# Attention block with a routed FFN on one core: the second batch's rotation moved to GpSimd, and the edges of stages and the end reordered

## The chip, the cores and the metric

One core of one Trainium2 chip. The time is the device time of one execution in microseconds (us), all loads, stores and on-chip work included. The engines are named as the profile names them: PE (TensorE matmuls) and PEld (its weight loads), DVE (VectorE), ACT (ScalarE), POOL (GpSimd) and SP (SyncE, which only issues DMAs here; SPq is its queue of DMA-issuing instructions).

## What is computed

Two batches of 1,024 tokens of width 128 go through attention (16 heads of 8 elements, rotary embedding, causal), a layer norm, a routed FFN of 4 experts (top 2) and a second layer norm, all in float32.

```python
Q = rope((x @ qw).reshape(batch, seq, 16, 8)); K = rope((x @ kw)...); V = (x @ vw)...
score = einsum('bhqd,bhkd->bhqk', Q, K) / sqrt(8); score = score - 1e10 * (1 - causal)
score = score - max(score); attn = einsum('bhqk,bhkd->bhqd', softmax(score), V)
x = layernorm(x + attn.reshape(batch, seq, 128) @ ow)
gates = top-2 of softmax(x @ router_w + router_b), renormalised
h = silu(x @ w1[e]) * (x @ w3[e]);  out = sum over e of gates[:, e] * (h @ w2[e])
x = layernorm(x + out)
```

## The kernel before

**Stages.** There are eight groups of four heads: groups 0 to 3 are the first batch, 4 to 7 the second. Stage s computes the score maxima of group s (40 "S" units, a matmul on PE followed by a row maximum on DVE) while the exponentials and the weighted sum of group s-1 run: "T" units are the transposed scores (PE), read by an exponential on ACT (L696) and, on the diagonal, a causal select on POOL (L574); "PV" units are the products with V (PE). Stage 0 (PROLOGUE) also holds part of its own group's T and PV. Stage 1 is FIRST, stages 2 to 7 follow STEADY_ORDER, and stage 8 (LAST) has no S. The order within a stage is one list of steps that all engines walk: in STEADY_ORDER `s`, `t`, `p`, `m`, `n` are an S, T, PV, MROWS and NORM step. Every engine executes its own part in that order and waits on semaphores.

**Maxima.** The maxima must be subtracted inside the T matmul. POOL splits them into three bf16 parts (split_max), PE turns them (MROWS), DVE copies them into max_rows, and SP sends them by four DMAs into extra rows of q_op (send_rows, L442). The first T unit of that half of the queries waits on these DMAs (rows_loaded). S units pass through a ring of three PSUM banks, so PE can be at most three units ahead of DVE.

**Projection and rotation.** x arrives in four chunks of 512 tokens, two for each batch. For each chunk q and k are projected (n = 0 to 7; n = 4 to 7 are the second batch). For each n, DVE multiplies the two projections by cosine and sine (turns_of), POOL adds them (sum_of_turns, L509), ACT writes the first bf16 part (first_part), DVE subtracts it (first_rest, L810), ACT writes the second (second_part), and POOL makes the third (third_part, L502). SP stores the parts, three DMAs for each n (L420), to a scratch area in DRAM in the six-fold form in which the groups load them (load_q, load_k). For n = 4 to 7 this is done by the steps P between the S units of the prologue, with the second batch's V.

**The end of attention and the FFN.** During LAST, steps C run the first layer norm and the router for chunk 0 (function between). For chunks 1 to 3 they are spread over the previous chunk's experts. An expert unit (16 for each chunk) is six matmuls of the two input products, silu on ACT, the product on DVE, a split of the hidden values into a high part (ACT) and a low part (POOL, L610), and three matmuls of the output product (L1206). The last layer norm and a store of 512 tokens close each chunk.

## Time and profile before

| | us |
|---|---|
| median of 3 runs | 436.07 |
| the three runs | 436.11, 432.88, 436.07 |
| the profiled execution, device time | 432.75 |
| its span in the trace | 430.7 |
| busy in the span: PE / DVE / ACT / POOL | 391.1 / 315.1 / 265.1 / 193.5 |

The profiled execution took 432.75 us, 2.05 us more than its span, and 3.3 us less than the median of the runs. By the trace, stage 0's last maxima are joined on DVE at 60.5 us, stage 7's at 241.7 us, the experts begin at 269.4 us and the last matmul of the FFN's products ends at 421.7 us. A row of the timeline gives the start, the duration, the engine and line, the operation, what it writes and reads, the count of merged instructions, and in brackets the idle time of the engine before it with what ended it. PEclk is TensorE's granted clock as a share of 2.4 GHz: 0.50 is 1.2 GHz.

### The profile page before, as it was taken

The numbers are of one execution on the slowest core, as the hardware profiler recorded it, in microseconds if no ns is written. First come the engines' busy times: TensorE is split into PE (matmuls) and PEld (weight loads), VectorE is DVE, ScalarE is ACT, GpSimd is POOL, SyncE is SP. The second block draws the span as 40 slices with busy tenths as digits, with TensorE's granted clock in tenths as the row PEclk, the third lists the DMA queues.
The fourth block names the chain that finished last, engine by engine and source line by source line (L and its number), as shares of the span: only waits on it lengthen the run. The fifth ranks groups of instructions, "written<-read, shape, count | busy, mean of one in ns | idle before, by whom it ended". The sixth has DMA issues, their size and how long they took to land.

```text
span 430.7 us, 7532 instructions
## 1 busy us (share of the span) xinstructions
PE 391.1 (91%) x2420; PEld 202.9 (47%) x2420; DVE 315.1 (73%) x1027; ACT 265.1 (62%) x377; POOL 193.5 (45%) x256
## 2 busy tenths in 40 slices
PE   4658769999999999999999888999999999999991
PEld 2243122232323323233232331788887887888770
DVE  3659888999999999999999543346576658656653
ACT  1233615687786867778687886566665656665550
POOL 7627611261343515235261322466565646655661
PEclk9959686999999999999999998999999999999996
DMA  6474841322213122131210000000000000000000
GB/s 216 153 203 91 286 115 23 75 53 57 52 22 89 39 70 51 25 93 22 74 35 3 1 3 2 0 2 1 2 1 24 2 1 24 2 1 3 24 0 24
DMA packets 45244, 21.13 MB, mean 49 GB/s; under 512 B 30995, under 2 KB 42899, under 8 KB 45206
## 3 DMA queue, kind: packets, MB, share of 16 engines
q1 hardware_dynamic: 44950, 20.47, 18.2%
q8 instruction: 19, 0.31, 0.3%
q10 hardware_dynamic: 256, 0.20, 0.2%
q14 instruction: 19, 0.16, 0.1%
HBM read 13.11 MB, written 7.35 MB: 47 GB/s over the span
## 4 chain that ended last, share of the span: by engine, by line
PE 70%; DVE 9%; ACT 5%; DMA 4%; issue 4%; POOL 3%; SPq 3%; ACTq 0%; POOLq 0%; DVEq 0%
PE o_bank L1127 14%; PE t_bank L1195 9%; PE bank L1084 9%; PE bank L1195 9%; PE t_bank L1206 9%; PE t_bank L1109 8%; PE small_bank L1084 5%; DMA q_op<-max_rows 3%; SPq L442 3%; ACT num L696 2%; DVE num L912 2%; POOL roped L509 1%; DVE num L985 1%; DVE x_w L850 1%; PE o_bank L1214 1%
## 5 line engine op out<-in xcount | busy, mean ns | idle before, releaser
L696 ACT ACTIVATE num<-t_bank 128x1024 f32<-128x1024 f32 (+2 forms) x160 | 142.8, 939 | 60.4 <-PE t_bank L1109 59.7
L610 POOL TENSOR_TENSOR hid_lo<-num,q_op 128x512 fp32r<-128x512 f32 x64 | 83.0, 1300 | 61.2 <-ACT q_op L749 60.0
L574 POOL TENSOR_SCALAR_AFFINE_SELECT num<-num 128x512 f32<-128x512 f32 x64 | 40.1, 636 | 120.7 <-ACT num L696 120.7
L1084 PE MATMUL bank<-k_op,q_op 128*128 128x512 bf16 (+7 forms) x256 | 71.8, 339 | 11.4 <-DMA q_op<-q_scratch 7.1
L1127 PE MATMUL o_bank<-num,v_op 128*32 128x512 f32 (+3 forms) x768 | 81.5, 503 | 0.1
L749 ACT ACTIVATE q_op<-num 128x512 fp32r<-128x512 f32 x64 | 40.5, 632 | 45.0 <-DVE num L985 44.5
L854 DVE TENSOR_REDUCE maxima<-bank 128x1 f32<-128x512 f32 x86 | 57.0, 684 | 2.6 <-PE bank L1084 1.6
L1109 PE MATMUL t_bank<-q_op,k_op 64*128 64x512 bf16 (+3 forms) x384 | 49.6, 337 | 4.3 <-ACTq L677 1.7
L1084 PEld LDWEIGHTS bank<-k_op,q_op 128*128 128x128 bf16 x256 | 21.2, 99 | 63.6 <-DVE maxima L854 23.4
L985 DVE TENSOR_TENSOR num<-bank,num 128x512 f32<-128x512 f32 x32 | 22.1, 691 | 30.7 <-ACT num L756 30.5
L850 DVE CUSTOM_DVE_ANT_0 mg_w<-bank,resid 128x256 f32<-128x256 f32 (+7 forms) x92 | 39.3, 447 | 4.7 <-PE bank L1084 3.8
L985 DVE TENSOR_TENSOR num<-t_bank,num 128x512 f32<-128x512 f32 x32 | 22.1, 690 | 27.3 <-ACT num L756 24.5
L1084 PE MATMUL small_bank<-k_op,q_op 128*128 128x512 bf16 (+6 forms) x128 | 38.7, 331 | 1.4 <-DVE maxima L854 1.1
L850 DVE CUSTOM_DVE_ANT_0 x_w<-small_bank,resid 128x64 f32<-128x64 f32 (+7 forms) x86 | 36.5, 443 | 3.4 <-PE small_bank L1084 1.6
L850 DVE CUSTOM_DVE_ANT_0 mg_t<-bank,resid 128x320 f32<-128x320 f32 (+7 forms) x78 | 35.1, 466 | 2.5 <-PE small_bank L1084 1.0
L1109 PEld LDWEIGHTS t_bank<-q_op,k_op 64*128 64x128 bf16 x384 | 13.9, 94 | 38.0 <-issue 15.5
L854 DVE TENSOR_REDUCE maxima<-small_bank 128x1 f32<-128x512 f32 x42 | 28.7, 683 | 1.3 <-PE small_bank L1084 0.9
L1127 PEld LDWEIGHTS o_bank<-num,v_op 128*32 128x32 f32 x768 | 15.9, 108 | 25.7 <-issue 22.4
L1195 PE MATMUL bank<-q_op,w_hi 128*128 128x512 f32 x64 | 26.8, 419 | 0.0
L1206 PE MATMUL t_bank<-q_op,w_hi 128*128 128x512 f32 x64 | 25.4, 396 | 0.9 <-POOL hid_lo L610 0.9
L1195 PE MATMUL t_bank<-q_op,w_hi 128*128 128x512 f32 x64 | 25.7, 401 | 0.2 <-DVE num L985 0.2
L1206 PE MATMUL t_bank<-hid_lo,w_hi 128*128 128x512 f32 x64 | 25.4, 397 | 0.0
(142 smaller groups left out, 629.2 us busy)
## 6 DMA issues: line engine op xcount, KB each, us to landing
q_op<-q_scratch SPq DMA_DIRECT2D x64, 48.0 KB
w_raw<-in_w_all SPq DMA_DIRECT2D x6, 512.0 KB, 4.0
k_op<-k_scratch SPq DMA_DIRECT2D x60, 48.0 KB, 1.9
xT<-in_x_feat SPq DMA_DIRECT2D x4, 256.0 KB, 5.9
q_op<-max_rows SPq DMA_DIRECT2D x64, 3.0 KB
out_tokens<-num SPq DMA_DIRECT2D x4, 256.0 KB, 2.3
q_scratch<-num SPq DMA_DIRECT2D x2, 384.0 KB, 2.8
k_scratch<-num SPq DMA_DIRECT2D x2, 384.0 KB, 2.8
```

Source lines behind the costliest of these rows:

```text
L574: pool.affine_select(out=tile, in_=tile, compare_op=ALU.is_ge, fill=0.0, base=0, pattern=[[0, GH], [1, P]], channel_multiplier=-1)\
L610: pool.tensor_tensor(hid_lo[:, m % HB, :], hid[:, m % HB, :], hid_hi[:, m % HB, :].bitcast(F32), ALU.subtract).then_inc(f_lo, 1)
L696: act.activation(num[:, t % PB, :, off:CH].rearrange("p (k i) t -> p i k t", i=2)[:, :, h:h + each, :], t_bank[k % TB][:, :, 0:each * (CH ...
L749: act.activation(hid_hi[:, m % HB, :], hid[:, m % HB, :], ACT.Copy).then_inc(f_hi, 1)
L850: ins = dve.tensor_tensor_reduce(masked_s[job % SB][:, at], ring(s, step)[:, at], causal[:, CH - width:CH], 1.0, LOWEST, ALU.add, ALU.max, ...
L854: ins = dve.tensor_reduce(maxima[:, half, pr, j:j + 1], ring(s, step)[:, at], AX.X, ALU.max)
L985: dve.tensor_tensor(hid[:, n % HB, :], bank[2 * (n % 2) + 1][:, :], silu_sb[:, n % 2, :], ALU.mult).then_inc(f_hid, 1)
L1084: ins = pe.matmul(ring(s, step)[:, i * width:(i + 1) * width], q_op[u][:, pr, j, :, :].rearrange("p i q -> p (i q)"), k_op[u][:, pr, lo:lo ...
L1109: ins = pe.matmul(t_bank[k % TB][:, i, (pr - h) * width:(pr - h + 1) * width] .rearrange("p (j q) -> p j q", q=QB), k_op[w][rows, pr, kt * ...
L1127: ins = pe.matmul(o_bank[h * QD:(h + 1) * QD, off:CH], v_op[w][:, kt, h, :], num[:, t % PB, h, off:CH], start=kt == 0, stop=kt == TI * (c ...
L1195: ins = pe.matmul(bank[2 * (n % 2) + w][:, :], ws[:, at], xs[ch], start=k == 0, stop=k == 2)
L1206: ins = pe.matmul(bank[4 + e % 2][:, :], ws[:, at], hs[:, m % HB, :], start=f == 0 and k == 0, stop=f == FT - 1 and k == 2)
```

## The change

- The rotation of n = 4 to 7 no longer uses DVE. ACT copies both projections to SBUF (copy_turns), and POOL alone does the seven operations that follow (late_block): two products, a sum, two casts and two subtractions. Each of these 28 is placed behind a given S unit of stage 0 (13) or stage 1 (15) by LATE_AT. For n = 0 and 1 the sum and the third part go from POOL to DVE.
- The projections of n = 4 and 5 and two of the V products come ahead of the prologue's first S unit, those of n = 6 and 7 and the last V product behind S units 5, 9 and 3.
- The stores of n = 4 to 7 go from the prologue to stage 2: six DMAs behind load_q in the middle, six at its end. x_tok is loaded at the end of stage 3 (it was in stage 0) into x_res, which serves as the buffer of late_block until then.
- FIRST has an order of its own; the prologue's T and PV units are two S units later. The tables' first half is loaded by ACT's queue.
- In LAST the copies that ACT made for steps C (L720, L726, L729, L733) are made by DVE, and L736's by POOL. The first three expert units (E) stand ahead of the last NORM.
- In the output product the matmul that reads the low part comes last of three. In the last chunk DVE makes the last low part; the last expert's copy, transposes and sum are done in halves; the last normalisation is shared by DVE and POOL, and its store by SP and ACT.

```diff
-PROJ_AT = (12, 14, 16, 18, 20)
-T_AT, PV_AT = (22, 24, 25, 27, 28, 30), (29, 31, 33, 35)
-V_AT = (3, 7, 11)
+PROJ_AT = (5, 9)
+V_AT = 3
+T_AT, PV_AT = (25, 27, 28, 30, 31, 33), (31, 33, 35, 37)
+LATE_STEPS = 7
+LATE_AT = [(0, at) for at in (2, 4, 6, 8, 14, 16, 18, 20, 22, 24, 29, 32, 36)] \
+    + [(1, at) for at in (2, 4, 6, 8, 10, 12, 14, 16, 18, 21, 24, 27, 30, 33, 36)]
-        plan.append(("NORM", NC - 1))
+        plan += [("E", n) for n in range(E_LAST)] + [("NORM", NC - 1)]     # E_LAST = 3
+FIRST_ORDER = "ssssmssssnsssststsstsstsssttsspssttsspmsttssspssttsspssttsspssnttppp"
-FIRST = steady_plan(STEADY_ORDER.replace("t", "", SEG_T[0] - T_END[0]).replace("p", "", TI), done=TI - 1)
+FIRST = steady_plan(FIRST_ORDER, done=TI - 1)
...
             def stage(plan, s, u, load=False):          # on sync
...
                         load_q(sp, s + 1, v, 0, range(GH))
+                        if s == 2:
+                            store(PROJ_FIRST)
+                            store(PROJ_FIRST + 1)
...
                         load_q(sp, s + 1, v, 1, range(GH))
                         load_k(sp, s + 1, v, 1)
+                        if s == 2:
+                            store(PROJ_FIRST + 2)
+                            store(PROJ_FIRST + 3)
+                        if s + 1 == NG:
+                            sp.dma_start(x_res[:, :, :], x_tok.rearrange("(t p) d -> p t d", p=P)).then_inc(ld_res, 16)
...
+            def late_block(k):                          # on gpsimd
+                n, r = PROJ_FIRST + k // LATE_STEPS, k % LATE_STEPS
+                at = n - PROJ_FIRST
+                cols = slice(n // 2 % NC * CH, (n // 2 % NC + 1) * CH)
+                by_cos, by_sin = late_turn[at]
+                if r == 0:
+                    pool.wait_ge(late_turned, at + 1)
+                    ins = pool.tensor_tensor(by_cos, by_cos, cos_sb[:, cols], ALU.mult)
+                if r == 1:
+                    ins = pool.tensor_tensor(by_sin, by_sin, sin_sb[:, cols], ALU.mult)
+                if r >= 2:
+                    pool.wait_ge(late_step, k)
...
+                if r == 2:
+                    ins = pool.tensor_tensor(by_cos, by_cos, by_sin, ALU.add)
+                if r in (3, 5):
+                    ins = pool.tensor_copy(rope_part(n, (r - 3) // 2), by_cos)
+                if r == 4:
+                    ins = pool.tensor_tensor(by_cos, by_cos, rope_part(n, 0), ALU.subtract)
+                if r == 6:
+                    ins = pool.tensor_tensor(rope_part(n, 2), by_cos, rope_part(n, 1), ALU.subtract)
...
+            def copy_turns(n):                          # on scalar
+                act.wait_ge(proj_ready, n + 1)
+                pair, at = 3 + 2 * (n % 2), n - PROJ_FIRST
+                act.activation(late_turn[at][0], bank[pair][:, :], ACT.Copy)
+                act.activation(late_turn[at][1], bank[pair + 1][:, :], ACT.Copy).then_inc(late_turned, 1)
...
+            copy_v(0)
+            copy_v(1)
+            first_part(2)
+            act.wait_ge(parts_stored[0], 2 * PARTS * 16)
+            act.wait_ge(ops_filled, 2)
+            load_k(act, 0, 0, 0)
+            second_part(2)
+            first_part(3)
+            copy_v(2)
+            act.wait_ge(ld_small, 16 * 2)
+            act.activation(ident_b[:, :], ident[:, :], ACT.Copy).then_inc(ident_cast, 1)
+            copy_turns(4)
+            second_part(3)
+            copy_turns(5)
+            copy_v(3)
...
             turns_of(0)                                 # on vector
-            for n in range(1, PROJ_FIRST):
+            sum_of_turns(0)
+            turns_of(1)
+            first_rest(0)
+            sum_of_turns(1)
+            third_part(0)
+            first_rest(1)
+            third_part(1)
+            for n in range(2, PROJ_FIRST):
                 turns_of(n)
-                first_rest(n - 1)
+                if n > 2:
+                    first_rest(n - 1)
...
+                if first and r == 0:                    # between(), on vector; r 1, 7 and 8 alike
+                    dve.wait_ge(job_read, SB + LAST_JOBS)
+                    dve.wait_ge(c_mgt, 1 + ch)
+                    dve.tensor_copy(mg_w[:, :].rearrange("p (i g r) -> p i g r", i=TI, g=NG),
+                                    merged[:, 1:1 + NG, 0:TI, :].rearrange("p g i r -> p i g r")).then_inc(c_mg, 1)
...
                     if f == 0:                          # experts(), on tensor
                         pe.wait_ge(f_eo, ch * E + e + 1)
-                    pe.wait_ge(f_lo, ch * UNITS + m + 1 + HB)
+                    pe.wait_ge(f_hi, ch * UNITS + m + 1)
                     at = slice(2 * E * F + m * P, 2 * E * F + (m + 1) * P)
-                    for k, (ws, hs) in enumerate(((w_hi, hid_hi), (w_hi, hid_lo), (w_lo, hid_hi))):
+                    for k, (ws, hs) in enumerate(((w_hi, hid_hi), (w_lo, hid_hi), (w_hi, hid_lo))):
+                        if k == 2:
+                            pe.wait_ge(f_lo, ch * UNITS + m + 1 + HB)
```

**SP's queue, the end of stage 2 and the start of stage 3.** Before, the maxima's rows (q_op<-max_rows) follow the loads for the next group at once:

```order
L378 DMA q_op<-zeros 3x8x64
L385 DMA k_op<-k_scratch 48x512 x4
L442 DMA q_op<-max_rows 3x8x64 [waits job_read]
L442 DMA q_op<-max_rows 3x8x64 x3
L374 DMA q_op<-q_scratch 48x8x64 [waits t_ready]
```

And now, at the same place:

```order
L406 DMA k_op<-k_scratch 48x512 x4
L442 DMA q_scratch<-by_sb 128x3x512 [waits late_ready]
L442 DMA q_scratch<-by_sb 128x2x512 [waits late_ready]
L442 DMA q_scratch<-roped 128x512 [waits late_ready]
L442 DMA k_scratch<-by_sb 128x3x512 [waits late_ready]
L442 DMA k_scratch<-by_sb 128x2x512 [waits late_ready]
L442 DMA k_scratch<-roped 128x512 [waits late_ready]
L464 DMA q_op<-max_rows 3x8x64 [waits job_read]
L464 DMA q_op<-max_rows 3x8x64 x3
```

Six stores of the second batch's last two blocks stand between the loads and the rows.

**POOL in stage 0, from the V layout to the first causal select.** Before (neg_max to max_part are the five small operations of split_max):

```order
L521 COPY v_op<-v_tok 128x32x8 [waits v_copied,v_cleared]
L539 TENSOR_SCALAR neg_max<-maxima 128x16 [waits job_read]
L540 CAST max_part<-neg_max 128x2x8 [waits split_step]
L541 TENSOR_TENSOR rest<-neg_max,max_part 128x16 [waits split_step]
L542 CAST max_part<-rest 128x2x8 [waits split_step]
L543 TENSOR_TENSOR max_part<-rest,max_part 128x2x8 [waits split_step]
L509 TENSOR_TENSOR roped<-by_sb 128x512 [waits split_step,part_ready2,turned]
L509 TENSOR_TENSOR roped<-by_sb 128x512 [waits part_ready2,turned]
L502 TENSOR_TENSOR x_res<-roped,x_res 128x512 [waits part_ready1]
```

Now:

```order
L576 COPY v_op<-v_tok 128x32x8 [waits v_copied,v_cleared]
L542 TENSOR_TENSOR x_res<-x_res,turns_sb 128x512 [waits late_turned]
L544 TENSOR_TENSOR x_res<-x_res,turns_sb 128x512
L550 TENSOR_TENSOR x_res<-x_res 128x512 [waits late_step]
L552 CAST x_res<-x_res 128x512 [waits late_step]
L594 TENSOR_SCALAR neg_max<-maxima 128x16 [waits job_read]
L595 CAST max_part<-neg_max 128x2x8 [waits split_step]
L596 TENSOR_TENSOR rest<-neg_max,max_part 128x16 [waits split_step]
L597 CAST max_part<-rest 128x2x8 [waits split_step]
L598 TENSOR_TENSOR max_part<-rest,max_part 128x2x8 [waits split_step]
L554 TENSOR_TENSOR x_res<-x_res 128x512 [waits split_step,late_step]
```

Four of POOL's new operations stand ahead of the first split of maxima, and none of them waits for DVE.

**PE at the end of LAST.** Before, the NORM's transposes (ident, o_sb), which wait for ACT's copy of the output, stand ahead of the experts:

```order
L1127 MATMUL o_bank<-num,v_op 32x128 [waits masked,t_exped]
L1127 MATMUL o_bank<-num,v_op 32x128 x3
L1146 MATMUL small_bank<-ident,o_sb 128x128 [waits job_read,o_copied]
L1146 MATMUL small_bank<-ident,o_sb 128x128 x3
L1195 MATMUL bank<-q_op,w_hi 128x512 [waits c_top,f_hid,c_lo]
```

Now the experts follow the last PV at once, and the transposes come behind three units of them:

```order
L1256 MATMUL o_bank<-num,v_op 32x128 [waits masked,t_exped]
L1256 MATMUL o_bank<-num,v_op 32x128 x3
L1330 MATMUL bank<-q_op,w_hi 128x512 [waits c_top,f_hid,c_lo]
L1330 MATMUL bank<-k_op,w_hi 128x512
L1330 MATMUL bank<-q_op,w_lo 128x512
```

## Rows read from the trace of the kernel before

**Rows 1.** Busy time by stretch: start:end, length, then each engine's busy (instructions).

```profile
60.50:86.50 26.00, 23.67 (x134) 6.66 (x134) 23.04 (x82) 12.82 (x14) 5.06 (x15) 0.80 0.30 75
86.50:112.30 25.80, 25.57 (x206) 8.16 (x202) 24.15 (x88) 19.50 (x23) 9.88 (x20) 1.00 0.25 54
241.80:269.40 27.60, 23.11 (x199) 8.54 (x198) 10.01 (x40) 21.76 (x30) 7.21 (x14) 0.94 0.01 2
269.40:421.70 152.30, 149.98 (x711) 121.10 (x709) 90.29 (x255) 92.82 (x162) 88.88 (x70) 1.00 0.02 6
```

**Rows 2.** Timeline of PE in stages 0, 1 and 3.

```profile
25.07 0.50 PE L1084 MATMUL bank<-k_op,q_op 128*128 128x64 bf16 x4 [7.13 <-DMA q_op<-q_scratch]
...
47.41 0.61 PE L1109 MATMUL t_bank<-q_op,k_op 64*128 64x512 bf16 x2 [1.74 <-ACTq L677]
...
62.21 0.30 PE L1136 MATMUL bank<-ident_b,max_part 128*48 128x128 bf16 x1 [2.05 <-POOLq L544]
...
119.52 0.61 PE L1109 MATMUL t_bank<-q_op,k_op 64*128 64x512 bf16 x4 [0.20 <-DMA q_op<-max_rows]
```

**Rows 3.** Timeline of DVE in stage 0.

```profile
13.10 1.61 DVE L810 TENSOR_TENSOR roped<-roped,num 128x512 f32<-128x512 f32 x1 [0.28 <-ACT num L654]
...
34.18 0.69 DVE L823 TENSOR_TENSOR by_sb<-t_bank,turns_sb 128x512 f32<-128x512 f32 x1
...
60.47 0.17 DVE L860 TENSOR_TENSOR maxima<-maxima 128x16 f32<-128x16 f32 x1
```

**Rows 4.** Timeline of POOL in stage 0.

```profile
11.13 1.27 POOL L509 TENSOR_TENSOR roped<-by_sb 128x512 f32<-128x512 f32 x1 [2.73 <-DVE by_sb L824]
...
17.89 1.15 POOL L502 TENSOR_TENSOR num<-roped,num 128x512 bf16<-128x512 f32 x1 [1.29 <-ACT num L650]
...
34.07 0.40 POOL L521 COPY v_op<-v_tok 128x256 f32<-128x256 f32 x1 [7.02 <-ACT v_tok L645]
```

**Rows 5.** Timeline of SP's DMA queue in stages 0, 3 and 4.

```profile
28.98 1.88 SPq L374 DMA_DIRECT2D q_op<-q_scratch  x4
...
40.67 3.12 SPq L442 DMA_DIRECT2D q_op<-max_rows  x4
...
113.06 1.72 SPq L385 DMA_DIRECT2D k_op<-k_scratch  x4
115.37 2.98 SPq L442 DMA_DIRECT2D q_op<-max_rows  x4
...
141.20 2.98 SPq L442 DMA_DIRECT2D q_op<-max_rows  x4
```

**Rows 6.** Issues of one line: count, then ns min/median/max of one.

```profile
L420 SPq DMA_DIRECT2D k_scratch<-num x6: 333/359/443, 17.0 to 27.1; - x6
```

**Rows 7.** One transfer in the view of DMA issues: KB each, us to landing.

```profile
x_res<-in_x_tok SPq DMA_DIRECT2D x1, 0.5 KB, 6.4
```

**Rows 8.** Single microseconds of Rows 1's view; last three: granted clock, DMA share, GB/s.

```profile
61.00:62.00 1.00, 0.00 (x0) 0.00 (x0) 0.39 (x4) 0.00 (x0) 0.72 (x4) 0.50 1.07 350
71.00:72.00 1.00, 1.00 (x8) 0.36 (x7) 1.00 (x2) 0.73 (x2) 0.40 (x1) 0.90 0.00 0
```

**Rows 9.** Timeline of PE in LAST.

```profile
245.39 0.66 PE L1166 MATMUL bank<-ident,mg_w 128*128 128x128 f32 x4 [1.36 <-ACT mg_w L720]
...
257.36 1.06 PE L1182 MATMUL bank<-rw,x_tw 128*128 128x4 f32 x8 [0.99 <-ACT x_tw L733]
...
269.00 0.66 PE L1146 MATMUL small_bank<-ident,o_sb 128*128 128x128 f32 x4 [0.71 <-ACT o_sb L705]
```

**Rows 10.** Waits from 272 to 420 us: total us, times, longest.

```profile
PE small_bank L1171 <- ACT mg_t L726: 1.1, 2, 0.6
```

**Rows 11.** Timeline of POOL, then of DVE, at the end.

```profile
419.39 1.27 POOL L610 TENSOR_TENSOR hid_lo<-num,q_op 128x512 fp32r<-128x512 f32 x1 [0.80 <-ACT q_op L749]
...
423.16 1.13 DVE L997 SCALAR_TENSOR_TENSOR num<-o_bank,gates,num 128x128 f32<-128x128 f32 x4 [3.48 <-PE o_bank L1214]
...
426.87 1.11 DVE L912 TENSOR_SCALAR num<-num,mv,rstd 128x128 f32<-128x128 f32 x4 [1.20 <-POOL rstd L614]
```

225 lines of the change are left out of this document (142 added, 83 removed).

## Prediction

> **What bounds the kernel now.** I read the busy time by stretch first, since the share over the whole span mixes stages with different limits. In a steady stage PE is busy 25.57 of 25.80 us, with DVE close behind at 24.15 [rows 1]. Nothing in stages 2 to 7 can gain unless PE's own work shrinks, and it doesn't. The experts are the same: PE 149.98 of 152.30 us [rows 1]. Time is open in four places. Stage 0 lasts to 60.5 us; its first score matmul waits 7.13 us for the loads of q, to 25.07, and its first T unit starts at 47.41 [rows 2]. In stage 1, PE is busy 23.67 of 26.00 us at a mean granted clock of 0.80 [rows 1], and DVE 23.04. In LAST, PE is busy 23.11 of 27.60 us [rows 1], and the waits named there are for ACT [rows 9]. At the end, a chain of short steps follows the last matmul [rows 11].
>
> **Stage 0, start.** The first rotation is a chain that passes from DVE to POOL, ACT, DVE, ACT and POOL. A sum takes 1.27 us on POOL [rows 4]; DVE operations of that size take about 0.68 [rows 3], except where one with two SBUF inputs met POOL's: 1.61 [rows 3]. Moving the two sums and third parts to DVE saves about 0.6 for the first sum, 0.5 for each third part, and the slowed subtraction; step by step I get the last part of n = 1 at 17.0 us instead of 19.0 (it began at 17.89 and took 1.15 [rows 4]). But ACT's queue now has two V copies and first_part(2) ahead of load_k, and first_part(2) waits for turns that DVE makes 2 us later than before. So k's loads move only from 20.8 to about 20.2, and the first S comes 0.6 us earlier, not 2. The fourth n is no earlier: second_part(3) stands behind copy_turns(4).
>
> **Stage 0, middle.** The four P steps with DVE work cost DVE 4 x 2 x 0.61 for turns (0.69 in the row, overlapping the next by 0.08 [rows 3]) and 4 x 0.7 for the subtractions, 7.7 us in all, between S units. That is removed. It does not become 7.7 us of gain, because of SP. From 28.98 us on SP issues six groups of four loads with no gap, each about 1.9 us, and reaches the maxima's rows at 40.67 [rows 5]. Nothing in the change shortens this: the loads start when n = 3 is stored, at 29.0 as before. The last row is issued at about 43.8 and lands 1.2 us later (in stage 3, 115.37 + 2.98 = 118.35, and PE starts at 119.52 [rows 2, 5]). So the first T unit can't start before 45.0. I expect PE and DVE to be through S25 at about 41.3 and to stall for 3.7 us; the T unit then starts at 45.0 instead of 47.41 with two S units more behind it (1.3 us). Together with a little idle time less behind, S40 is read at 56.1 instead of 60.5 [rows 3]: **-4.4 us**, with 0 and -7 as the ends (nothing; all 7.7 but 0.7).
>
> **POOL's 28 new operations.** 20 have two inputs, 1.15 to 1.27 us each [rows 4]; 8 are casts, which the trace has only smaller: 0.40 for 256 elements [rows 4], and at most a two-input operation's 1.15. I take 0.65, near twice 0.40 less the fixed part. The sum is 20 x 1.2 + 8 x 0.65 = 29 us. From 27.3 us to the end of stage 1 there are about 53 us, with 12 us of other work for POOL (5.06 in stage 1 [rows 1] and about as much again, with V and the selects, in stage 0). 41 of 53 fits, and most blocks wait for nothing, so POOL runs ahead of its place. They are hidden: 0 us. DVE's S operations read PSUM and one SBUF tile, as its turns do, and those kept 0.69 us [rows 3].
>
> The Trainium skill (SBUF — State Buffer, "Who interferes with whom") says that a DVE operation holds up GpSimd's reads where both its inputs are in SBUF. The row of 1.61 us agrees; by that rule the S units leave POOL alone, which keeps the rival on POOL below small.
>
> **Stage 1.** MROWS behind four S units instead of two hides PE's 2.05 us wait for POOL's split [rows 2], since S3 and S4 give DVE about 1.3 us more to do meanwhile. T starts after S12, when its rows (4.2 us from the copy) have landed. DVE then bounds the stage: 23.04 us of work [rows 1], 0.55 for the NORM moved in, some 1 of unavoidable gaps. 26.2 becomes about 24.5: **-1.7** (0 to -2.5).
>
> **The moved stores.** In the middle of stage 2 SP has time for six more issues. At its end it has not. A store's issue takes 0.36 us [rows 6], 0.41 with its gap, so six take 2.5 us. SP had 0.59 us free between the end of load_k (113.06 + 1.72) and the rows at 115.37 [rows 5], and then 0.20 us of PE waiting was left at the T unit [rows 2]: PE was already waiting for these rows. So everything beyond 0.59 is added: **+2.0** (0 to +4, as 1.57 MB, two n of six copies of 128 x 512 x 2 bytes, also move at the 350 GB/s that the row of 61 us shows, 4.5 us [rows 8]). PE has nothing later to win it back from.
>
> In stage 4 x_tok's load stands at the same place. By issue alone it would cost 0.3 us: one issue of up to 0.9, less 0.59. But it takes 6.4 us to land [rows 7]. Issued at 140.6 it lands at 147.0; the rows, issued at 141.20 [rows 5], landed by the pattern of stage 3 at 145.3. I take **+1.5** (+0.3 to +2.5), near the later bound, because 1 MB spreads over all DMA engines ahead of the rows.
>
> The Trainium skill (DMA: Bandwidth & Descriptors, "Queues, rings and completion order") says that on each engine the descriptors of a queue are consumed in ring order. By it the rows start only behind x_tok's data, 1.7 us late; without it, 0.3. No row of this trace has the two back to back.
>
> **LAST.** PE waits 1.36 us for the copy of mg_w, 0.99 for x_tw and 0.71 for the output's copy [rows 9], 3.06 us; ACT makes those copies between exponentials. DVE is busy 10.01 of 27.60 us [rows 1] and takes its copies at once. ACT loses 3 us of work. The other waits make up the 4.5 us of PE's idle time; some turn into waits for exponentials. Without the 0.71, which belongs to the next step: **-3.4** (-2 to -5; the last 1.6 is what its mean clock of 0.94 lost over 27.6 us [rows 1]). E ahead of NORM removes the 0.71 wait, and silu and the first product follow earlier; NORM's transposes are still executed: **-0.9** (-0.5 to -1.3).
>
> **Experts.** The order of three matmuls is worth nothing where PE is saturated. The move of mg_t's copy in front of the hidden split removes PE's 1.1 us [rows 10]: **-0.8** (0 to -1.1).
>
> **End.** The last low part took POOL 419.39 to 420.66 [rows 11]; on DVE it is 0.69 behind a sum, to 420.4, and the matmul that needs it is now the third: -0.8. Halves let the sum of 1.13 us [rows 11] start about 0.65 earlier. The last normalisation, 1.11 us [rows 11], becomes 0.56 beside POOL's half, at -0.5 with the shorter stores: **-2.0** (-1.2 to -2.6).
>
> **Sum.** -4.4 - 1.7 + 2.0 + 1.5 - 3.4 - 0.9 - 0.8 - 2.0 = -9.7 us, against the profiled execution's 432.75: 423.05. The median of the runs is 3.3 us above that execution, with nothing in one trace to say why. I put the same difference on the median: 436.07 - 9.7 = **426.4**. A difference of 1% (4.4 us) is about what a measurement of this kernel can tell from none.
>
> **Rivals.**
> - *Half clock after the stalls in stages 3 and 4.* In stage 1 PE idled 2.05 us and the clock was at half from 61 to 71 us [rows 2, 8]. There DVE set the pace, so it cost little; in a stage where PE is busy 99% ten such microseconds cost up to 5. Against it: waits of 1.36 and 0.99 us in LAST cost only a share of 0.06 [rows 1]. One such fall: 426.4 + 5 = 431.4. Chance 0.15, for 429 to 434.
> - *Stage 0 gains nothing.* The longer stall puts PE at half clock (after waits of this kind it was there at 61 us [rows 8]) and the T units crawl: 426.4 + 4.4 = 430.8. Chance 0.08. For it: T can start only 2.4 us earlier. Against: DVE has 9 us of S units left there, at any clock.
> - *POOL becomes the bound: the slower side.* The place is stages 0 and 1: selects and splits stand behind the new blocks, and PV and the rows wait for them. 53 - 12 = 41 us are free, 1.47 a block; beyond that mean each block's excess is paid 28 times. From 1.97 a block it costs 14 us and eats all of the gain and 1% more: 440. For it: an addition took 1.61 on DVE against POOL [rows 3], so slow meetings exist; against: POOL's own rows are at 1.15 to 1.27. Chance 0.04.
> - *More than the sum.* Fewer waits keep PE at full clock in stages 0 and 1 and in LAST, which has 1.6 us at stake, and stage 4's load doesn't delay the rows: 422. Chance 0.13.
>
> The forecast has 0.60, for 423 to 430. The range leaves out a tenth on each side at most: it takes in rival four (less its tail) and most of the first two, 419.5 to 432. Faster by over 1% (below 431.7): 0.59 of the forecast, 0.13, 0.07 and 0.06 of the first two, 0.85. Within 1%: 0.11. Slower: 0.04.
>
> **What would show it.** Right: T's first unit at 45 us behind a PE wait of 3 to 4 us for q_op<-max_rows; DVE's join of stage 0 at 56; PE waits of about 2 us for q_op<-max_rows in stages 3 and 4 and none elsewhere; no PE wait for mg_w or x_tw in LAST; the experts beginning some 4 us sooner after stage 7's join. Wrong: a T unit in stage 0 that waits for ACT or POOL, POOL busy over 9 tenths there, or no wait in stage 3, which would put the time some 3 us lower.

## The result and the profile after

The changed kernel took 430.98 us, the median of ten executions from 430.11 to 432.40. The kernel before took 435.37 us beside it, the median of ten from 432.88 to 436.18. The ratio is 0.9924, with a 95% interval from 0.9900 to 0.9948. The change is a gain of 3.3 us by the ratio (the two medians alone lie 4.4 us apart), under the 1% that the prediction named as the bound of "faster". The forecast was 426.4.

The profiled execution took 431.6 us with a span of 429.9 and a mean clock of 0.962 (before: 432.75, 430.7 and 0.955). The spans of the two traces therefore differ by only 0.8 us. This small difference is made of large gains and large losses that stand against each other. To see it, I cut both traces at the same events: the instruction of DVE that joins the maxima of a stage (L860 before, L961 after), and the first matmul of the experts.

```
stretch                                before    after   change   predicted
start to join of stage 0                60.47    59.29    -1.18        -4.4
stage 1                                 26.21    24.67    -1.54        -1.7
stage 2                                 25.84    25.62    -0.22         0
stage 3                                 25.82    30.50    +4.68        +2.0
stage 4                                 25.83    30.46    +4.63        +1.5
stages 5 to 7                           77.55    77.50    -0.05         0
join of stage 7 to first expert matmul  27.70    23.20    -4.50        -3.4, and -0.9 for E
first expert matmul to the end         161.28   158.66    -2.62        -0.8 and -2.0
sum                                                       -0.80        -9.7
```

Two notes on the table. A second trace of the changed kernel (after_p1, below) divides the first two rows differently, with 2.3 us gained in stage 0 and 0.7 in stage 1; their sum is the firmer number, 2.7 us here and 3.1 there. And the first expert matmul now stands ahead of NORM's transposes, which took 0.4 us before it (269.00 [rows 9] to 269.42), so 0.4 of the 4.50 us has only moved into the last row.

These are the stretches of the changed kernel in the columns of [rows 1], and two of stage 0 where the first T unit stands:

```profile
40.00:48.00 8.00, 1.66 (x7) 0.37 (x6) 1.91 (x7) 0.83 (x1) 1.98 (x2) 0.66 0.24 51
48.00:54.00 6.00, 6.00 (x32) 1.26 (x34) 3.64 (x10) 3.79 (x6) 3.03 (x5) 0.60 0.01 0
59.30:83.96 24.66, 23.04 (x132) 7.24 (x138) 23.48 (x86) 12.93 (x15) 20.63 (x30) 0.86 0.18 42
109.58:140.08 30.50, 26.31 (x201) 8.19 (x202) 24.45 (x88) 19.71 (x24) 9.89 (x20) 0.94 0.35 97
140.08:170.54 30.46, 26.34 (x201) 8.15 (x202) 24.44 (x88) 19.71 (x24) 9.89 (x20) 0.94 0.33 80
248.05:271.24 23.19, 21.35 (x195) 8.23 (x194) 12.59 (x44) 18.39 (x24) 7.77 (x15) 1.00 0.01 2
271.24:421.06 149.82, 149.52 (x712) 121.77 (x712) 90.62 (x256) 93.91 (x163) 87.60 (x69) 1.00 0.02 6
```

Read the third row first. POOL is at 20.63 us in stage 1, where it had 5.06 [rows 1], and yet the stage is shorter: DVE's 23.48 us fill it. Then the fourth and fifth: PE did the work of a steady stage in 30.5 us; it was busy for 26.3 of them, a part of that at half clock. In the first row, all engines are mostly idle together, from 40 to 48 us. Who is late, the timeline of PE names (it answers to [rows 2]):

```profile
46.52 0.61 PE L1238 MATMUL t_bank<-q_op,k_op 64*128 64x512 bf16 x2 [6.34 <-DMA q_op<-max_rows]
...
61.06 0.30 PE L1265 MATMUL bank<-ident_b,max_part 128*48 128x128 bf16 x1 [0.60 <-POOLq L599]
...
120.05 0.60 PE L1238 MATMUL t_bank<-q_op,k_op 64*128 64x512 bf16 x4 [3.88 <-DMA q_op<-max_rows]
...
150.48 0.60 PE L1238 MATMUL t_bank<-q_op,k_op 64*128 64x512 bf16 x4 [3.81 <-DMA q_op<-max_rows]
```

The last of these rows is the third wait for the same kind of transfer, in stage 4. The wait for POOL's split has become 0.60 us from 2.05 [rows 2]. All three large waits end with the transfer of the maxima's rows, so the next view is SP's queue (it answers to [rows 5]):

```profile
42.04 3.11 SPq L464 DMA_DIRECT2D q_op<-max_rows  x4
...
110.11 1.71 SPq L406 DMA_DIRECT2D k_op<-k_scratch  x4
111.87 0.96 SPq L442 DMA_DIRECT2D q_scratch<-by_sb  x2
112.87 0.72 SPq L442 DMA_DIRECT2D q_scratch<-roped  x1
113.64 1.24 SPq L442 DMA_DIRECT2D k_scratch<-by_sb  x2
114.92 0.95 SPq L442 DMA_DIRECT2D k_scratch<-roped  x1
115.91 2.96 SPq L464 DMA_DIRECT2D q_op<-max_rows  x4
...
142.54 1.80 SPq L507 DMA_DIRECT2D x_res<-in_x_tok  x1
144.39 3.67 SPq L464 DMA_DIRECT2D q_op<-max_rows  x4
```

The six moved stores keep SP from 111.87 to 115.87. Counted from the join before them, the rows are issued 6.33 us later (115.91 - 109.58), and before the change it was 2.85 us (115.37 - 112.52) [rows 5]. In stage 4 one load holds the queue for 1.80 us, and then the four rows take 3.67 us to issue instead of 2.98 [rows 5]. After the wait of stage 3 the granted clock falls to the lower of its two levels, 1.2 GHz, for three microseconds (single microseconds, last three columns clock, DMA share, GB/s):

```profile
120.00:121.00 1.00, 0.95 (x6) 0.23 (x6) 0.00 (x0) 0.52 (x1) 0.00 (x0) 1.00 0.54 85
121.00:122.00 1.00, 1.00 (x9) 0.20 (x8) 0.98 (x3) 1.00 (x2) 0.20 (x1) 0.52 0.47 72
...
123.00:124.00 1.00, 1.00 (x7) 0.22 (x9) 0.79 (x6) 0.55 (x1) 0.58 (x2) 0.50 0.08 16
```

The stage is 4.68 us longer and its wait 3.68 us longer than before (3.88 less the 0.20 in [rows 2]): the clock's share is 1.0 us.

POOL's new operations, grouped by line from 20 to 84 us (busy us, mean ns, then idle time before them), cost about what was estimated (1.2 us for an operation with two inputs, 0.65 for a cast):

```profile
L544 POOL TENSOR_TENSOR by_sb<-by_sb,turns_sb 128x512 f32<-128x512 f32 x2 | 2.5, 1272 | 0.0
...
L552 POOL CAST by_sb<-by_sb 128x512 bf16<-128x512 f32 x4 | 2.4, 610 | 0.2
```

The end of the changed kernel (it answers to [rows 11]) has DVE's half, POOL's half and the store that follows POOL's:

```profile
425.84 0.66 DVE L1010 TENSOR_SCALAR num<-num,mv,rstd 128x128 f32<-128x128 f32 x2 [1.19 <-POOL rstd L670]
```

```profile
425.91 1.65 POOL L675 TENSOR_SCALAR num<-num,mv,rstd 128x128 f32<-128x128 f32 x2 [0.18 <-POOL rstd L670]
```

```profile
427.60 0.41 ACTq L861 DMA_DIRECT2D out_tokens<-num  x1
```

A tile of the normalisation takes 0.83 us on POOL and 0.28 on DVE (1.11 for four [rows 11]). The last row but one is thus the longer half, and it sets when the output leaves.

### The profile page after: what moved, and what is told of

The parts are those of the page before. It is cut to its first block, busy times and chain, and to the rows that moved or that the text cites. A ratio compares the mean times of both kernels' runs of the same rounds, so it can differ in the third digit from the quotient of the medians.

```text
span 429.9 us, 7520 instructions
## 1 busy us (share of the span) xinstructions
PE 387.0 (90%) x2398; PEld 202.4 (47%) x2420; DVE 311.4 (72%) x1022; ACT 262.0 (61%) x373; POOL 207.7 (48%) x274
## 4 chain that ended last, share of the span: by engine, by line
PE 70%; DVE 11%; SPq 6%; DMA 5%; issue 3%; ACT 2%; POOL 2%; ACTq 0%; POOLq 0%; DVEq 0%
PE o_bank L1256 13%; PE bank L1330 10%; PE t_bank L1330 10%; PE t_bank L1343 10%; PE bank L1215 8%; PE t_bank L1238 7%; PE small_bank L1215 4%; DMA q_op<-max_rows 3%; SPq L464 3%; DVE mg_w L951 2%; DVE x_w L951 2%; DVE maxima L955 2%; DVE mg_t L951 2%; PE o_bank L1352 2%; SPq L406 1%
## 5 line engine op out<-in xcount | busy, mean ns | idle before, releaser
L666 POOL TENSOR_TENSOR hid_lo<-num,q_op 128x512 fp32r<-128x512 f32 x63 | 81.7, 1301 | 57.9 <-ACT q_op L825 56.7
L1215 PE MATMUL bank<-k_op,q_op 128*128 128x512 bf16 (+7 forms) x241 | 66.0, 332 | 4.3 <-DMA q_op<-q_scratch 1.6
L955 DVE TENSOR_REDUCE maxima<-bank 128x1 f32<-128x512 f32 x83 | 55.5, 685 | 3.7 <-PE bank L1215 2.5
L951 DVE CUSTOM_DVE_ANT_0 x_w<-small_bank,resid 128x384 f32<-128x384 f32 (+7 forms) x82 | 35.8, 454 | 8.3 <-PE small_bank L1215 6.7
L1215 PE MATMUL small_bank<-k_op,q_op 128*128 128x512 bf16 (+7 forms) x121 | 37.6, 338 | 2.8 <-DVE maxima L955 0.9
L951 DVE CUSTOM_DVE_ANT_0 mg_t<-bank,resid 128x448 f32<-128x448 f32 (+7 forms) x80 | 35.8, 464 | 2.9 <-PE small_bank L1215 1.4
L955 DVE TENSOR_REDUCE maxima<-small_bank 128x1 f32<-128x512 f32 x45 | 30.8, 684 | 8.2 <-PE small_bank L1215 7.3
L1330 PE MATMUL t_bank<-q_op,w_hi 128*128 128x512 f32 x64 | 25.7, 401 | 0.0
L1215 PEld LDWEIGHTS small_bank<-k_op,q_op 128*128 128x128 bf16 x127 | 11.2, 98 | 30.7 <-DVE maxima L955 10.1
```

What stands on the lines that cost most here:

```text
L666: pool.tensor_tensor(hid_lo[:, m % HB, :], hid[:, m % HB, :], hid_hi[:, m % HB, :].bitcast(F32), ALU.subtract).then_inc(f_lo, 1)
L951: ins = dve.tensor_tensor_reduce(masked_s[job % SB][:, at], ring(s, step)[:, at], causal[:, CH - width:CH], 1.0, LOWEST, ALU.add, ALU.max, ...
L955: ins = dve.tensor_reduce(maxima[:, half, pr, j:j + 1], ring(s, step)[:, at], AX.X, ALU.max)
L1215: ins = pe.matmul(ring(s, step)[:, i * width:(i + 1) * width], q_op[u][:, pr, j, :, :].rearrange("p i q -> p (i q)"), k_op[u][:, pr, lo:lo ...
L1330: ins = pe.matmul(bank[2 * (n % 2) + w][:, :], ws[:, at], xs[ch], start=k == 0, stop=k == 2)
```

## Experiments

**The theory** after the traces: the change did what it set out to do on every engine, and lost most of it on SP's queue. At three places DMA issues stand in order ahead of the rows that PE waits for: the loads of group 1 in stage 0, six stores in stage 3, one load in stage 4. **The rivals**: the data of those transfers and not the order of the issues (it is under way beside the rows wherever the issues stand); the clock; and that another engine would be late next, so that no edit of the queue gives more than a part.

**One cause at a time.** Three kernels, each the changed one with one edit. Only the kernel before ran beside each of them, so a difference from the changed kernel's 430.98 us is one between series; the stages in the traces are the firmer reading. The first moves the stores of blocks 6 and 7:

```
 if step == ("T", 1, 0, 0, 0):            # stage 3
-    wait parts_stored[2], parts_stored[3]
+    wait parts_stored[2]
     load_q(sp, s + 1, v, 0, range(GH))
+    if s + 1 == NG: store(PROJ_FIRST + 2); store(PROJ_FIRST + 3)
 if step == ("END",):
+    if s + 1 == NG: wait parts_stored[3]
     load_q(...); load_k(...)
-    if s == 2: store(PROJ_FIRST + 2); store(PROJ_FIRST + 3)
```

> The changed kernel with the six stores of blocks 6 and 7 moved from the end of stage 2, where the rows of stage 3 queue behind them (rows issued at 115.91 us, a PE wait of 3.88 us, half clock behind it, stage 3 taking 30.5 us and not 25.8), to the middle of stage 3 behind the q loads. Theory A: the lateness of the rows is what stage 3 costs, all of it. Then stage 3 reads 25.9 us, the wait falls to about 0.4 us, and the kernel ends 4.7 us earlier: 426.3 us, 0.9815 of before. Rival B: SyncE's queue is as late as before with the stores gone, since the q and k loads of stage 4 already fill it (before: rows issued 1.6 us behind the last load): then the wait stays over 2 us and the gain is under 2 us. Rival C: the traffic of the stores moves the wait into the next loads: q of stage 4 lands late, and the time goes back by 2 to 4 us in stage 4.

Measured 427.62 us, ratio 0.9834 (0.9776 to 0.9893). Stage 3 read 25.81 us. Stage 4 still had its wait, 3.99 us, and read 30.64. Theory A holds at its place: stage 3 is back at what it was before the change. The whole kernel gained a little less than the 4.7 us expected, 4.2 us in the traces (425.7 for 429.9) and 3.4 by the medians; in its trace stage 7 read 26.29 us, where four k loads took 2.73 us to issue and PE waited 0.87 for the rows behind them. Of what rival C feared, the stores' traffic delaying the next loads, stage 4 shows at most 0.2 us (30.64 for 30.46), though the four k loads at the end of stage 3 took 2.62 us here and 1.71 in the changed kernel's first trace.

The second moves one load:

```
 load_k(sp, s + 1, v, 0); load w_raw      # ("T", 1, TI, 0, 0)
+if s == NG: load x_res
...
-if s + 1 == NG: load x_res               # ("END",)
```

> The changed kernel with the load of x_tok (512 KB) moved from the end of stage 3 to the middle of stage 4, behind the load of w_raw; nothing else is changed. Theory A: what stage 4 costs (30.46 us and not 25.8; PE wait 3.81 us and half clock for three us) comes from the rows that are issued 1.8 us later and whose transfer shares the DMA engines with that load (3.67 and 3.07 us for rows that took 2.98). Then the kernel ends 4.6 us earlier: 426.4 us, 0.982 of before, and stage 4 reads 25.9 us. Rival B: only the 1.8 us of issue count and the clock does not come back, a gain under 2 us. Rival C: in the middle of the stage the 512 KB delay the k loads of stage 5, and stage 5 is longer by 1 to 3 us.

Measured 427.54 us, ratio 0.9858 (0.9805 to 0.9911). (The load is of 1 MB, 2,048 tokens of 128 float32, and not of the 512 KB that the expectation names.) Stage 4 read 25.82 us, as expected. The kernel gained less than 4.6 us, 3.1 in the traces, and in its trace stage 5 read 26.74 instead of 25.85:

```profile
167.86 2.44 SPq L406 DMA_DIRECT2D k_op<-k_scratch  x4
```

The four k loads ahead of stage 5's rows took 2.44 us to issue instead of 2.04 in the changed kernel, and the rows behind them came late. Stage 5 is where rival C put its cost, and x_tok's data were still landing at 169.0. As a rule it does not hold: in the six other kernels below with the load at this place stage 5 read 25.92 to 25.95 us five times and 26.26 once. A slow issue of k loads came up in other traces too, with this load elsewhere (below).

The third changes the order in stage 0:

```
-sp.wait_ge(ops_filled, 4)
-for c in range(NC): load_q(sp, 1, 1, c, ...); load_k(sp, 1, 1, c)
 send_rows(0, ..., 0)
+sp.wait_ge(ops_filled, 4)
+for c in range(NC): load_q(sp, 1, 1, c, ...); load_k(sp, 1, 1, c)
```

> The changed kernel with the first rows of maxima sent before the 12 loads of group 1 on SyncE's queue and not behind them. The cast of the rows was done at 35.5 us, SyncE issued them at 42.04, they landed at 45.15 and more, and PE waited 6.34 us for them. Theory A: the queue is the bound of stage 0: the rows go out at about 36 us, the wait of 6.34 us falls under 1 us, the loads of group 1, which no one needs before stage 1, are hidden, and the kernel ends 5 to 6 us earlier: about 425.5 us, 0.98 of before. Rival B: PE then waits for another (exp of ScalarE, masks of GpSimd, or group 1's operands land too late for the first scores of stage 1), and under 2.5 us is gained. Rival C: the half clock after the stall is the larger part, and more than 6.5 us is gained.

Measured 425.39 us, ratio 0.9798 (0.9744 to 0.9851): 5.6 us under the changed kernel. SP's queue and PE in its trace:

```profile
35.62 3.12 SPq L459 DMA_DIRECT2D q_op<-max_rows  x4
```

```profile
40.29 0.61 PE L1237 MATMUL t_bank<-q_op,k_op 64*128 64x512 bf16 x2
```

The rows go out 6.4 us earlier, the first T unit comes at 40.29 instead of 46.52 and waits for no one, and the join is at 52.23 instead of 59.29. That is 7.1 us in stage 0; the loads of group 1, which now begin at 38.78 and not at 33.46, are hidden.

**All three together.**

> The three edits of the first runs together: stores of blocks 6 and 7 in the middle of stage 3, x_tok's load in the middle of stage 4, the first rows ahead of group 1's loads. Theory: three separate places of one mechanism, rows of maxima queued on SyncE behind DMA issues; each alone took one stage down (stage 0 by 7.1 us, stages 3 and 4 by 4.7 each), so together they add: 431 - 7.1 - 4.7 - 4.6 = 414.6 us, 0.953 of before, all stages from 2 on at 25.6 to 25.9 us and the last join at 231.7 us. Rival: with one stall gone the others shrink (fewer conflicts on the DMA engines), so the three overlap and the sum is under 12 us: above 419 us.

Measured 414.27 us (413.96 to 415.09), ratio 0.9556 (0.9518 to 0.9595). The stages in the trace read 50.54 for stage 0, then 24.97, 25.60, 25.78, 26.10, 25.94, 25.86, 25.80. The expected time was 414.6. The three places are separate and add, and little is late behind them: stage 4 is 0.3 us over a steady stage, where the four k loads ahead of its rows took 2.56 us to issue. This kernel beats the one before by 4.4% and the changed one by 3.7% by the two ratios, 3.9% by the two medians. The experiments that follow go on from it, but for the one on the kernel before.

**Half the dose.** Only the stores of block 6 stand ahead of stage 3's rows again.

```
 if step == ("T", 1, 0, 0, 0) and s + 1 == NG:
-    store(PROJ_FIRST + 2); store(PROJ_FIRST + 3)
+    store(PROJ_FIRST + 3)
 if step == ("END",) and s == 2:
+    store(PROJ_FIRST + 2)
```

> The kernel with the three edits, but only block 7's three stores stay in the middle of stage 3; block 6's three stand again at the end of stage 2, ahead of the rows. Half the dose of what cost stage 3 4.7 us. Theory A (every microsecond that SyncE issues ahead of the rows is passed on to PE, once the 0.59 us of slack are gone): three stores take 1.7 us (0.96 + 0.72 for block 6 in the trace of the changed kernel), PE waits 1.4 to 1.6 us, and stage 3 is 1.5 us longer than with all six moved, a little more if the clock falls: 27.2 to 27.8 us. Rival B (the clock is the cost, and falls after any wait of over a microsecond for the same time): stage 3 reads 28.5 us or more. Rival C (the traffic of the stores is what delays the rows, 1.57 MB): wait nearer 2.3 us.

```profile
110.53 0.61 PE L1239 MATMUL t_bank<-q_op,k_op 64*128 64x512 bf16 x4 [1.36 <-DMA q_op<-max_rows]
```

Stage 3 read 26.99 us, 1.2 more than with all six moved. The rows were issued 4.03 us behind the join (106.39 - 102.36), and 2.85 with all six moved, so they were 1.18 us later; that is the 1.77 us that the two DMAs of block 6 took with their gaps, less the 0.59 of slack. PE's wait grew by 1.0 (from 0.37), and the clock was granted in full behind it. So issue time ahead of the rows, beyond the slack, is passed on one to one, and here only the longer wait brought the clock down. Theory A; its lower end of 27.2 was 0.2 high. The time, 417.10 us, lies 2.8 above the full edit; 1.8 of these are stage 0, whose join came at 52.31 in this trace and 50.54 in the other, with the same code there.

**Order or traffic.** x_tok's load directly behind the rows of stage 4, meant to have both under way together:

```
 send_rows(s, step, u if step[1] == 0 else v)
+if (s, step[1]) == (NG, NC - 1): load x_res
```

> The kernel with the three edits, but x_tok's load stands directly behind the rows at the head of stage 4 instead of in its middle. Behind the changed kernel's cost in stage 4 stand two causes: the 1.8 us that SyncE took to issue it ahead of the rows, and the transfer that shares the DMA engines with the rows. Here the first is gone and most of the second stays (its data and the rows' are under way together). Theory A (order on the queue decides): stage 4 reads 25.8 to 26.2 us as with the load in the middle. Rival B (sharing the engines decides): the rows land late though issued in time, PE waits over 1.5 us for them, and stage 4 reads 27.5 us or more.

```profile
129.57 2.97 SPq L459 DMA_DIRECT2D q_op<-max_rows  x4
133.08 0.86 SPq L483 DMA_DIRECT2D x_res<-in_x_tok  x1
```

Measured 414.59 us, ratio 0.9554 (0.9523 to 0.9584); stage 4 read 25.83, PE's wait for the rows was 0.19 us. The order on the queue decides: theory A. The run doesn't bear out the thought that both are under way together, since the T unit started at 133.71, 0.6 us after the load was issued; what rows would lose to a load that is not ahead of them in the same queue stays untested. The load slowed the issues that stood behind it: the next q load took 1.66 us to issue, where 0.3 is usual, and no one waited for it. The Trainium skill (DMA: Bandwidth & Descriptors, "Queues, rings and completion order") says that on each DMA engine the descriptors of a queue are consumed in ring order. These runs agree: behind the load the rows were late, ahead of it they were not. In the changed kernel the rows of stage 4 went out 1.45 us later against the join (4.31 us for 2.86) and took 0.69 us longer to issue, and PE waited some 3.6 us more, which leaves about 1.5 us for rows that landed behind x_tok's data. The traces show that part directly. The T unit there came 2.42 us after the issue of the rows had ended (150.48 - 148.06), and here 1.17 (133.71 - 132.54). Wherever the load stood right ahead of the rows (the changed kernel twice, two of the three kernels with one edit, and the kernel of the next experiment), the T unit started 0.5 to 0.9 us after x_tok had landed: at 150.48 where it was issued at 142.54 and took 7.3 us to land.

**The rival on stage 0: was the queue the bound before, too?** The kernel before, with rows ahead of the loads of group 1 as in the third experiment:

> The kernel of before, with the one edit that gave most in stage 0 of the changed kernel: first rows ahead of the loads of group 1. Theory: there DVE and ScalarE, not the rows, set the first T unit (its wait at 47.41 us names ScalarE's queue, and the rows had been issued at 40.67), so the same edit gives under 1 us, 434 us, ratio 0.998 to 1.002: the rows became the bound only with the change. Rival: the rows bound stage 0 before too, and the edit gives 2 to 5 us.

Measured 436.92 us, ratio 1.0085 (1.0052 to 1.0119): slower.

```profile
63.74 0.88 SPq L455 DMA_DIRECT2D x_res<-in_x_tok  x1
64.68 3.31 SPq L437 DMA_DIRECT2D q_op<-max_rows  x4
```

```profile
71.21 1.03 PE L1108 MATMUL t_bank<-q_op,k_op 64*128 64x512 bf16 x4 [3.54 <-DMA q_op<-max_rows]
```

The first T unit came at 47.17 with the same wait of 1.74 us for ACT's queue as in [rows 2]: no gain, as expected, and the join of stage 0 came at 61.60 us, later than in any of the five traces of the kernel before (60.47 to 60.95). But in this kernel the stores of batch 2 follow on SP, and everything behind them moved too: x_tok's load from 57.95 to 63.74, and the rows of stage 1, now right behind it, from 62.86 to 64.68. The load took 6.7 us and landed at 70.4; the T unit came at 71.21, 3.2 us after the issue of its rows had ended (67.99), so about 2 us more were lost behind x_tok's data, by the mechanism of stage 4 above. Stage 1 went from 26.21 to 30.06 us. So the same edit loses 0.85% before the change and gives 1.3% after it, where those stores and x_tok's load have left stage 0. The expectation of 0.998 to 1.002 was missed because it asked only what the edit does at its own place.

**What LAST's copies gave.** The five copies of C back on ACT:

```
-DVE: between(r in 0, 1, 7, 8, first=True) copies mg_w, mg_t, x1_hi, x1_tw;  POOL: r == 9 copies x1
+ACT: if step[0] == "C": between(0, 0, 0, step[1], first=True)
```

> The kernel with the three edits, and the five copies of LAST's chain (mg_w, mg_t, x1_hi, x1_tw, x1) back on ScalarE as before. Theory: those moves gave most of LAST's 4.5 us (before: waits of 1.36 us for mg_w and 0.99 us for x_tw, behind exps in ScalarE's order; the prediction put 3.4 us on them). Against the three edits alone this is 3 to 4.5 us longer, from the last join to the first expert matmul, with both waits back in PE's row. Rival: the early experts (E ahead of the last NORM) gave it, and this costs under 1.5 us.

Measured 418.63 us, ratio 0.9655 (0.9617 to 0.9692), 4.4 us above the kernel with the three edits; join to first expert matmul 27.92 us instead of 23.02.

```profile
235.32 0.66 PE L1281 MATMUL bank<-ident,mg_w 128*128 128x128 f32 x4 [1.36 <-ACT mg_w L792]
...
248.82 1.06 PE L1297 MATMUL bank<-rw,x_tw 128*128 128x4 f32 x8 [0.99 <-ACT x_tw L805]
```

```profile
238.00:241.00 3.00, 3.00 (x19) 1.01 (x18) 1.60 (x6) 0.00 (x0) 0.23 (x1) 0.52 0.02 5
...
252.00:256.00 4.00, 3.81 (x25) 0.54 (x18) 1.52 (x7) 3.18 (x6) 0.64 (x1) 0.68 0.00 0
```

Both waits are back to the hundredth. PE's waits from the join of stage 7 to the end come to 4.4 us, against 2.3 without the edit; the rest of the 4.9 is the clock, low from 238 to 241 and again in 252 to 256, and full throughout with the copies on DVE.

**E ahead of NORM.** PE's wait for c_top with its two credits then stands behind the stage:

```
-E_LAST = 3
+E_LAST = 0
```

> The kernel with the three edits, and the first three steps of the experts back behind the last NORM and its copy instead of ahead of them (nothing else). Theory: the early steps cover one wait of PE of about 0.9 us for the last normalisation, as the prediction has it: this is 0.7 to 1.2 us longer. Rival: they cover the router's chain too (PE waits for c_top in any case, so the order is worth nothing): within 0.3 us. Second rival: SiLU and products start later for the whole first chunk and it costs 2 us or more, which would be where the 2.4 us of the expert phase came from.

```profile
254.72 0.66 PE L1275 MATMUL small_bank<-ident,o_sb 128*128 128x128 f32 x4 [0.71 <-ACT o_sb L778]
```

The wait of 0.71 us is the one of [rows 9], and the first expert matmul comes 1.13 us later against the join. The 1.13 us are this wait and 0.4 us of transposes, which stand ahead of the boundary in one order and behind it in the other; from the first expert matmul to the end it is 0.4 us less here. In the traces the early steps are thus worth 0.7 us, the wait alone. The time was 416.16 us, ratio 0.9596 (0.9557 to 0.9635), 1.9 above; 0.4 of it is in the trace ahead of the edit, as the join of stage 7 came later. Between 0.7 and 1.5 us, the term of 0.9 us stands. With the copies on ACT, the early steps brought nothing (27.92 us of LAST with them, 27.70 before without): the two edits don't simply add.

**The tables.** Their first half back on SP behind the first x:

```
-load_table(act, 0)
-    if ch == 1: load_table(sp, 1)
+    if ch < NC: load_table(sp, ch)
```

> The kernel with the three edits, and cos/sin for the first 512 tokens loaded on SyncE's queue behind the first 512 tokens of x, where they stood before, and not at the head of ScalarE's. Theory: the transfers at 1.1 and 1.5 us took the DMA engines from wqk and x, and the first matmul came 0.95 us later (6.84 us for 5.89): here it comes at 5.9 us and all that follows is 0.9 us earlier, against the kernel with the three edits alone. Rival: the first rotation then waits for the tables (DVE's L903 begins later), as before the change (13.1 us): no gain, or a loss up to 1 us.

```profile
6.17 5.46 PE L1167 MATMUL t_bank<-xT,wqk 128*128 128x512 f32 x6 [6.17 <-DMA xT<-in_x_feat]
```

Measured 414.13 us, ratio 0.9550 (0.9519 to 0.9581): the same. The first matmul came 0.52 us sooner than without the edit (6.69), not at the 5.9 expected, but DVE then waited 0.63 us for PE at 12.67 and the join came at 51.20, not before 50.54. Where the tables are loaded is worth nothing that can be told from the scatter of stage 0.

**The last normalisation** whole on DVE, with one store:

```
-POOL: tiles 2, 3 of z -> last_z;  ACT: wait last_z, store;  DVE: tiles 0, 1;  SP: store of half
+DVE: tiles 0 to 3;  SP: one store
```

> The kernel with the three edits, and the last normalisation back on DVE alone with one store from SyncE. In the changed kernel POOL's half takes 1.65 us (425.91 to 427.56) and its store is issued at 427.60; DVE's half is ready at 426.5. DVE does four tiles in 1.1 us. Theory A: the split on two engines is a loss, since POOL needs 0.83 us for a tile that DVE does in 0.28: this is 0.3 to 0.6 us shorter. Rival B: one store of all four tiles lands later than two halves on two queues, which gives the half microsecond back: same within 0.2 us.

```profile
409.97 1.12 DVE L999 TENSOR_SCALAR num<-num,mv,rstd 128x128 f32<-128x128 f32 x4 [1.19 <-POOL rstd L669]
```

```profile
411.11 0.37 SPq L515 DMA_DIRECT2D out_tokens<-num  x1
```

Measured 415.24 us (414.28 to 416.02), ratio 0.9567 (0.9540 to 0.9594). From veps to the end it is 5.20 us here (408.60 to 413.8) and 5.41 in the kernel with the three edits (406.99 to 412.4); the join of stage 7 was 1.57 us later in this trace, before the edit begins. Rival B, or at most 0.2 us for theory A: the split on POOL and its second store were worth nothing.

**Where executions of one kernel differ.** Open was why the trace on which the sum was made lay 3.3 us under the median, and so whether -0.8 us (traces) or -4.4 (medians) is the change. Four executions of the kernel before were traced again, and one more of the changed kernel.

> The kernel of before, once more. The profiled run on which the prediction's sum was made took 432.75 us and nine further runs took 434.8 to 436.2. Theory: the ledger of that one trace is some 2.5 us short of an ordinary run, so this trace spans about 2.5 us more, in one or two places (stage 0, the handovers between the stages, LAST or the end), and those places are where an ordinary run of the changed kernel must be compared. Rival: the missing 2.5 us lie evenly over the span or outside it, and every stage reads within 0.3 us of the first trace.

> The kernel of before again, traced, for the question why the prediction's trace (432.75 us) lies under the median of the runs (435 to 436). Theory: what varies is stage 0 alone, from the landing of the first x to the join (traces of one kernel there read 50.3 to 52.3 us, and the later stages agree within 0.1 us): an execution of 435 us shows the join 2 to 3 us later than 60.5. Rival: single late rows in the steady stages, a wait of 0.8 to 1.3 us here and there, as seen in some traces.

> As the first of this call: one more execution of the kernel before. Theory: its time less the last join's time is 189 us as in the first trace, and the difference from 432.75 us is in the time of the first join.

> As the first of this call: a third execution of the kernel before, same expectation.

> The changed kernel again, traced. Theory: stages 3 and 4 read 30.5 us each again, since the cause is the order on SyncE's queue and no accident; the time is 430 to 432.5 us, and its spread is stage 0's. Rival: the 0.8 us between the first two traces and the 4.4 us between the medians differ because the first trace of this kernel was a slow one: then this one ends 2 us earlier.

The four took 432.87, 433.70, 432.68 and 433.67 us. Joins of stage 0: 60.84, 60.95, 60.57 and 60.87, against 60.47 in the first trace. Two of the four have one stage of 26.35 and 26.38 us instead of 25.83, with a wait of 0.94 us for the rows:

```profile
139.36 2.80 SPq L385 DMA_DIRECT2D k_op<-k_scratch  x4
142.20 2.98 SPq L442 DMA_DIRECT2D q_op<-max_rows  x4
```

The k loads ahead of the rows took 2.80 us to issue instead of 1.72 [rows 5]. So both the theory and the rival hold, each for a part: up to 0.5 us in stage 0, 0.5 for a slow issue. They reach 433.7 and not the 435 to 436 that other executions took; none of that length was caught in a trace. Beside the later kernels the kernel before had medians of 434.63, 433.36 and 433.41 us, so the 3.3 us between trace and median on which the forecast leaned was not a fixed trait of the kernel. The changed kernel's second trace took 433.13 us, above the first, and not 2 us below as the rival would have it: stage 3 read 30.57 again and stage 4 32.28, as its k loads took 2.86 us PE's wait for the rows was 4.49 us and the clock was at half from 151 to 157, about 2 us beyond the length of the wait. What the change is worth in an ordinary execution stays at what the medians say, 0.76% with its interval; the last 2 us of the scatter of the kernel before are not explained.

## Why the prediction was wrong, step by step

The direction and the places were right: T's wait for the rows, the two waits in stages 3 and 4 and none elsewhere, no wait for mg_w or x_tw, POOL hidden. The range, 419.5 to 432, held the time. The forecast was 4.6 us too good, and in the traces the sum was 8.9 us too good. Three terms failed, all of them rows of maxima behind other DMAs on SP's queue: stage 0 by 3.2 us, the moved stores by 2.7 and x_tok's load by 3.1. In each the prediction had the mechanism, rows issued late or landing late, and mis-sized it.

**The moved stores: the wrong row.** The step took 0.36 us for a store's issue from [rows 6], which are stores of blocks 0 to 3. The trace of before also had the very stores that move:

```profile
45.49 2.25 SPq L420 DMA_DIRECT2D k_scratch<-x_res  x3
47.79 1.25 SPq L420 DMA_DIRECT2D q_scratch<-x_res  x2
49.08 0.93 SPq L420 DMA_DIRECT2D q_scratch<-w_raw  x1
```

They take 0.62 to 0.93 us each. Six took 4.00 us with their gaps after the change. With that, the step's own working (less 0.59 of slack) gives 3.4 us; PE's wait grew by 3.68. The step's upper end of +4 was exceeded because the clock's 1.0 us came on top, which the prediction had as a rival of its own at 5 us: the mechanism came true in both stages at a fifth of the price (at two fifths in stage 4 of the second trace). The half-dose run shows that the step's rule, everything beyond the slack is added, is right.

**x_tok's load: two terms of three.** The step counted its issue as up to 0.9 us less the slack, and the wait for its data. The issue took 1.80 us, and the rows went out 1.45 us later; their own issue grew by 0.69, which the step left out, and the data added 1.3 to 1.5. I chose 1.5 us near a bound of 2.5, and 4.6 were lost, 1.0 of them the clock. The order on the queue is the cause (the run with the load behind the rows).

**Stage 0: the bound was found and mis-sized.** "Nothing in the change shortens this" was right; the queue was the bound. But the rows were issued at 42.04 and not at 40.67, since the loads of n = 3 began 0.65 us later (29.63) and one group of k loads took 2.59 us. T came at 46.52, not 45.0. From there to the join the prediction had 11.1 us and it took 12.8, at a mean clock of 0.60 from 48 to 54 us, behind a stall of 6.34 us and not 3.7. The rival "stage 0 gains nothing" had this mechanism and was given 0.08. With the rows first, the join is 8.2 to 10.2 us earlier than before the change: stage 0 then gives more than the 7.7 us of work that were taken off DVE, and in the changed kernel the queue kept most of it. No run parts that work from the other edits of stage 0. The start gave less than its term: the first S unit came at 24.95 us for 25.07, not 0.6 earlier, as the first matmul came 0.95 us later (6.84 for 5.89); the tables on ACT's queue were part of that, by the run above.

**Stage 1, POOL, LAST, experts, end: right.** Stage 1 gave 1.54 of 1.7 in the first trace and 0.7 in the second. POOL's casts took 0.61 us for an estimated 0.65, its sums 1.27 for 1.2, all hidden. LAST gave 4.50 of 4.3 for both its terms (4.1 without the transposes that left it), and the copies' share was larger than 3.4, some 4.9 by the run with them on ACT, because the clock came with the waits: the upper end, "what its mean clock of 0.94 lost", is where it landed. Experts and end together gave 2.62 of 2.8 (3.0 with the transposes set aside); they can't be parted at the boundary where I had, since the wait for the last low part ends inside the expert phase. In the end term, 0.5 us were put on the split of the normalisation, and it is worth nothing.

**The sum.** Adding 3.3 us to the result, since the median stood so far above the trace, took part of the error back by chance. The three terms as they were measured (4.68 for 2.0, 4.63 for 1.5, -1.18 for -4.4) turn the -9.7 into -0.7, which is the difference of the traces.
